# Keys of a pair of batches in one group of 512 columns, and context split a tile ahead, in a cross-attention, self-attention and expert kernel

## What is computed

```
x = x + cross_attention(layernorm(x), ctx, ctx)          # 16 heads of 16
x = x + self_attention(layernorm(x))                     # rms norm, rope, sigmoid weights
x = x + experts(layernorm(x))                            # top 1 of 8, capacity 160

q = layernorm(x) @ Wq.T + bq;  k = ctx @ Wk.T + bk;  v = ctx @ Wv.T + bv
cross_attention = softmax(q k^T) v @ Wo.T + bo
experts: logits = tokens @ gate_w + gate_b; expert = argmax; position = running count
         gelu(tokens @ w1 + b1) @ w2 + b2, times the gate's probability
```

## Time and profile before

| | |
|---|---|
| median of 3 runs (lowest to highest) | 1187.33 us (1187.31 to 1187.4) |
| the profiled execution: time, span | 1189.84 us, 1187.6 us |
| busy: TensorE, its weight loads | 1096.9 us (92%), 923.9 us (78%) |
| busy: VectorE, ScalarE, GpSimd | 896.2 us (75%), 809.6 us (68%), 252.5 us (21%) |
| scores of slot 0 start: tile 1, 4, 18, 30 | 48.34, 145.54, 592.50, 975.30 us |
| granted TensorE clock, 145.5 to 1007.2 us | 1.00 (2.4 GHz) |
| keys, 1536 matmuls of 256 columns | 216.3 us busy, 291 ns each |
| ScalarE's copy of keys, 256 of 128x256; of values, 128 of 128x512 | 484 ns each; 625 ns each |

### The profile page before, as it was taken

The page is one execution under the profiler, slowest core; times in us unless marked ns, Lnnn a source line. Parts: engine busy times, 40 slices in busy tenths (PEclk is TensorE's granted clock), DMA queues, the critical chain, the costliest instruction groups (busy, mean ns, idle before and its releaser), DMA issues. The chain is left out here.

```text
span 1187.6 us, 42401 instructions
## 1 busy us (share of the span) xinstructions
PE 1096.9 (92%) x16905; PEld 923.9 (78%) x16905; DVE 896.2 (75%) x2654; ACT 809.6 (68%) x2441; POOL 252.5 (21%) x565
## 2 busy tenths in 40 slices
PE   6899999999999999999999999999999999863996
PEld 5678788877878888888888878878888887742996
DVE  5768888888888888888888888888888888741121
ACT  5667777777777777777787777777777777621221
POOL 0001221222222222222222222222122222222111
PEclk9889999999999999999999999999999999955999
DMA  5443411222212211121111111112111211001573
GB/s 134 115 109 101 163 51 55 62 63 59 60 56 58 60 42 57 49 57 58 51 42 55 55 56 56 56 56 57 42 51 51 53 56 34 15 10 34 171 250 109
DMA packets 71922, 82.26 MB, mean 69 GB/s; under 512 B 16987, under 2 KB 50732, under 8 KB 71728
## 3 DMA queue, kind: packets, MB, share of 16 engines
q1 hardware_dynamic: 65280, 75.19, 21.6%
q0 software_dynamic: 3200, 3.71, 0.9%
q10 hardware_dynamic: 3248, 0.66, 0.3%
HBM read 64.79 MB, written 16.56 MB: 68 GB/s over the span
## 5 line engine op out<-in xcount | busy, mean ns | idle before, releaser
L721 ACT ACTIVATE prob<-score,nmx 128x257 f32<-128x257 f32 x512 | 236.2, 476 | 124.0 <-DVE nmx L929 124.0
L393 PE MATMUL kps<-ctx_p,wk_p 128*128 128x256 f32 x1536 | 216.3, 291 | 0.2 <-issue 0.2
L403 PE MATMUL vps<-wv_p,ctx_p 128*128 128x256 f32 x1536 | 213.5, 289 | 0.0
L393 PEld LDWEIGHTS kps<-ctx_p,wk_p 128*128 128x128 f32 x1536 | 196.9, 193 | 18.2 <-issue 15.5
L929 DVE TENSOR_REDUCE nmx<-score 128x2 f32<-128x514 f32 x256 | 165.2, 687 | 59.9 <-PE score L423 59.9
L403 PEld LDWEIGHTS vps<-wv_p,ctx_p 128*128 128x128 f32 x1536 | 193.1, 192 | 0.9
L940 DVE TENSOR_SCALAR prob<-prob,rsum 128x256 f32<-128x256 f32 x512 | 165.0, 365 | 9.1
L1255 POOL TENSOR_TENSOR rstd<-ve,const 128x1 f32<-128x1 f32 x64 | 53.0, 829 | 497.4 <-DVE ve L983 276.2
L439 PE MATMUL score<-const,prob 128*128 128x128 f32 x1024 | 148.9, 279 | 6.6 <-DVE prob L940 4.6
L439 PEld LDWEIGHTS score<-const,prob 128*128 128x128 f32 x1024 | 112.8, 142 | 22.5 <-DVE prob L940 21.8
L739 ACT ACTIVATE ctx_p<-ctxT,nlast 128x256 fp32r<-128x256 f32 x256 | 119.6, 536 | 0.4 <-issue 0.4
(11 more groups left out here) (150 smaller groups left out, 1748.0 us busy)
## 6 DMA issues: line engine op xcount, KB each, us to landing
ctxT<-in_ctxT SPq DMA_DIRECT2D x128, 257.0 KB, 3.0
w<-in_w SPq DMA_DIRECT2D x16, 1024.0 KB, 8.6
xq<-in_x SPq DMA_DIRECT2D x32, 128.0 KB, 2.1
xr<-in_x SPq DMA_DIRECT2D x32, 128.0 KB, 2.4
qbd<-qkT SPq DMA_DIRECT2D x256, 16.0 KB, 1.8
out<-row SPq DMA_DIRECT2D x32, 128.0 KB, 2.0
slots<-row SPq DMA_DIRECT2D x10, 257.0 KB, 5.7
x_a<-slots SPq DMA_DIRECT2D x8, 129.0 KB, 2.1
```

Source lines behind the costliest of these rows:

```text
L393: last = mm(kps[:, c, :], wk_p[:, x, n, c * P:(c + 1) * P], ctx_p[:, g, y, n, :], start=(n, x) == (0, LO), stop=(n, y) == (C - 1, LO))
L403: last = mm(vps[:, c, :], ctx_p[:, g, x, n, c * P:(c + 1) * P], wv_p[:, y, n, :], start=(n, x) == (0, LO), stop=(n, y) == (C - 1, LO))
L721: last = af(prob[:, m, :], score[:, m, 0:S], ACT.Exp, bias=nmx[:, m:m + 1], scale=1.0, accum_out=esum[:, m:m + 1])
```

## The change

Keys: one group now holds a pair of batches and one chunk, six matmuls with 512 columns. Slots 0 and 1 make the two chunks of this tile's second pair, slots 2 and 3 those of the next tile's first pair. ScalarE evacuates each with one operation. The context parts have a slot for each of four batches, and in slot j the parts of batch j of the next tile are made. The context loads go out correspondingly earlier, and on SyncE's queue they stand behind the loads of x, one of the two behind the qbd copies. ScalarE's copy `y2T` moves ahead of the copy of the values, and VectorE's `choose` behind `norm_x_apply` and `probT`.

```diff
-        ctx_p = sb("ctx_p", [P, 2, 2, C, SM], F32R)
+        ctx_p = sb("ctx_p", [P, 2, C, TB, SM], F32R)
-        kT = sb("kT", [P, 2, C, S])
+        kT = sb("kT", [P, 2, C, 2, S])
-        kps, vps = ps("kps", [P, C, SM]), ps("vps", [P, C, D])
+        kps, vps = ps("kps", [P, 2 * SM]), ps("vps", [P, C, D])
...
 SyncE
-                sp.wait_ge(s["ctx_parts"], floor0(TB * t + 2 * r - 2))
+                sp.wait_ge(s["ctx_parts"], floor0(TB * (t - 1) + 2 * r + 2))
...
             load_ctx(0, 1)
+            load_ctx(1, 0)
...
-                if q:
-                    load_ctx(i + 1, 0)
...
                 if once(i):
+                    load_ctx(1, 1)
                     load_weights()
...
-                if q:
-                    load_ctx(i + 1, 1)
+                if i <= T - 3:
+                    load_ctx(i + 2, 0)
                 if s1:
...
                     send_diag(lambda h: qkT[HD * h:HD * (h + 1), 0:C, :],
                               lambda h: qbd2[HD * h:HD * (h + 1), :, h, :], "qbd2_in")
+                if i <= T - 3:
+                    load_ctx(i + 2, 1)
...
 TensorE
+            def keys(t, r, c):
+
+                p = 2 * t + r
+                pe.wait_ge(s["ctx_parts"], 2 * p + 2)
+                pe.wait_ge(s["k_evac"], 2 * p + c)
+                for n in range(C):
+                    for x, y in PASSES:
+                        last = mm(kps[:, :], wk_p[:, x, n, c * P:(c + 1) * P],
+                                  ctx_p[:, y, n, 2 * r:2 * r + 2, :].rearrange("p j s -> p (j s)"),
+                                  start=(n, x) == (0, LO), stop=(n, y) == (C - 1, LO))
+                last.then_inc(s["k_done"], 1)
...
-            keys(0, 0)
+            keys(0, 0, 0)
             pe.wait_ge(s["wparts_done"], 2)
             values(0, 0)
+            keys(0, 0, 1)
...
-                    if ahead:
-                        keys(ta, ja)
+                    if xa and (j < 2 or q):
+                        keys(*((i, 1) if j < 2 else (i + 1, 0)), j % 2)
...
 ScalarE
+            def keys(t, r, c):
+                p = 2 * t + r
+                act.wait_ge(s["k_done"], 2 * p + c + 1)
+                act.wait_ge(s["s_done"], floor0(2 * (2 * p - 2)))
+                af(kT[:, r, c, :, 0:SM], kps[:, :].rearrange("p (j s) -> p j s", j=2), ACT.Identity, bias=b_k[:, c:c + 1],
+                   scale=1.0).then_inc(s["k_evac"], 1)
...
             context_hi(0, 0)
+            context_hi(0, 1)
...
-            keys(0, 0)
-            context_hi(0, 1)
+            keys(0, 0, 0)
+            context_hi(0, 2)
             values(0, 0)
+            keys(0, 0, 1)
+            context_hi(0, 3)
...
-                    if xa and (j < 2 or q):
-                        context_hi(*((i, j + 2) if j < 2 else (i + 1, j - 2)))
+                    if q:
+                        context_hi(i + 1, j)
...
+                    if j == 3 and s2:
+                        copy_rows(y2T[:, :, :], spare2_c, "y2t_ps", t2, "y2T_done")
                     if ahead:
                         values(ta, ja)
...
-                    if j == 3 and s2:
-                        copy_rows(y2T[:, :, :], spare2_c, "y2t_ps", t2, "y2T_done")
...
 VectorE
                     normalise(i, 0)
+                if q:
+                    norm_x_apply(i + 1)
+                if xa:
+                    probsT(i, 0)
                 if i >= 3:
                     choose(t2 - 1)
-                if xa:
-                    probsT(i, 0)
-                if q:
-                    norm_x_apply(i + 1)
...
-                    context_lo(i, 3)
+                if q:
+                    context_lo(i + 1, 1)
```

More of the change, by code:

```diff
@@ L383, in project_queries @@
                 last.then_inc(s["q_ps"], 1)
[L385 to L394, removed]
+            def keys(t, r, c):
[7 more added lines that the diff above has]
+                                  start=(n, x) == (0, LO), stop=(n, y) == (C - 1, LO))
                 last.then_inc(s["k_done"], 1)
             def values(t, j):
-                b, g = TB * t + j, j % 2
+                b = TB * t + j
                 pe.wait_ge(s["v_evac"], b)
@@ L424, in scores @@
                                   qz[rows, half, e, j, :, :].rearrange("p h q -> p (h q)"),
-                                  kT[rows, b_slot(j), e, :], start=True, stop=True)
+                                  kT[rows, j // 2, e, j % 2, :], start=True, stop=True)
                         if e and m % 2:
@@ L723, in exps, with context_hi @@
                     last.then_inc(s["exp_done"], 1)
[L725 to L739 removed]
+            def keys(t, r, c):
[4 more added lines that the diff above has]
+                   scale=1.0).then_inc(s["k_evac"], 1)
+            def context_hi(t, j):
+                b, r = TB * t + j, j // 2
+                act.wait_ge(ctx_in[r], 16 * C * (t + 1))
+                act.wait_ge(s["v_done"], floor0(b - TB + 1))
+                for c in range(C):
+                    last = af(ctx_p[:, HI, c, j, :], ctxT[:, r, c, j % 2, 0:SM], ACT.Identity, bias=nlast[:, c, b:b + 1], scale=1.0)
                 last.then_inc(s["ctx_hi"], 1)
@@ L1103, in _ @@
             context_lo(0, 0)
+            context_lo(0, 1)
             dve.wait_ge(s["bq_in"], 16 * 4)
@@ L1113, in _ @@
             v.tensor_copy(row[:, 2 * D + 1:ROW], k["sentinel"]).then_inc(s["slots_init"], 1)
-            context_lo(0, 1)
             dve.wait_ge(s["wkv_in"], 16 * 5)
-            v.tensor_copy(kT[:, :, :, SM:S], b_k[:, :].unsqueeze(1).unsqueeze(3).to_broadcast([P, 2, C, 1])
-                          ).then_inc(s["bk_done"], 1)
+            for r in range(2):
+                v.tensor_copy(kT[:, r, :, :, SM:S], b_k[:, :].unsqueeze(2).unsqueeze(3).to_broadcast([P, C, 2, 1])
+                              ).then_inc(s["bk_done"], 1)
+            context_lo(0, 2)
+            context_lo(0, 3)
             def body(i, half):
```

42 lines of the change are left out of this document (15 added, 27 removed).

## The result

The changed kernel takes 1167.37 us (median of 5 runs, 1165.84 to 1169.57), the kernel before in the same session 1187.33 us (1186.1 to 1190.12). The ratio is 0.983 [0.981, 0.985]: 20 us faster, where 29.6 were forecast. The time lies in the range of 1150 to 1173, the forecast of 1158 is 9 us too low.

The account below looks back on a forecast made before the run. TensorE was taken to set the pace, standing still twice a tile, for y2T and probT. Terms 19.5 + 14.2 + 1.1 + 0.8 - 2 - 4 = 29.6 us off 1187.3 gave 1157.7, say 1158 us; range 1150 to 1173.

Parts of the forecast that it names:

- The rows' copy: Slot 3: y2T copied ahead of the values ends the gate matmuls' wait, 0.65 us a tile, 30 tiles, 19.5 us.
- The choice: Slot 0: routing choice behind probT ends the weighted values' wait, 0.49 us for 29 tiles, 14.2 us; slot 1 slack 0.04.
- Wide keys: Six 512-column matmuls for twelve of 256: 0.035 us a tile, counting in slot 2 only, 1.1 us (0 to 5).
- The start: Before the first scores: added context parts and keys, weights behind one more context load, 4 us lost (1.5 to 6).
- The last tile: Slot 2 there has no keys; TensorE's wait before the transposes' second half shrinks, 0.8 us gained.
- The qbd copies: Their reader comes earlier, leaving 0.5 us of cover; late landings in 4 tiles cost 2 us (0 to 6).
- the rival built on the Trainium skill's sustained 131 ns a matmul: Keys in slot 2: 512-column matmuls take half the row's time, saving 14 us, 1144 us; chance 0.03.
- the qbd copies become the bound: Rival: the eighth copy lands at 593, not 592, in most tiles, losing 0.4 us a tile, 1170 us; chance 0.07.
- The range: Whole kernel: terms' bounds give 1150 to 1165 us, widened to 1150 to 1173 to reach the first two rivals.
- What would show it: Period 30.8 us, both waits gone; wrong over 31.3, transposes waiting over 0.1 in slot 1, or six matmuls under 1.3.
- stuck ahead of the rows' copy: Rival, slot 3: ScalarE waits for transposes arriving over 0.28 us late; at 2 us late, 1209 us; chance 0.05.
- no VectorE wait took either place: Denies the rival that a VectorE wait in slot 1 gives back slot 0's gain, 1172 us; chance 0.12.

Follow-up runs that it names:

- moves_only: The kernel before with only the two moves (y2T ahead of the values' copy, choice behind probT), keys and context as before: 1169.84 us, ratio 0.984.
- undo_rows_copy: The changed kernel with the rows' copy y2T put behind the values' copy again, the rest of the change kept: 1168.1 us, ratio 0.982 to the kernel before.

## Why the prediction was right, and where it was not

- *The rows' copy, 0.65 us a tile: right.* Slot 3 went from 8.84 to 8.19. 0.49 of it is the move (moves_only), 0.16 the shorter keys' copy, which the prediction had counted into the same step: `qz` stands 0.57 behind the keys' copy, not 0.50, and it still sufficed. That the move itself buys nothing in the time (undo_rows_copy) is the copies' doing, below.
- *The choice, 0.49: right.* Slot 0 went from 7.82 to 7.33, and nothing came back in slot 1: the 0.04 us of slack held (clean slot 1 went from 7.56 to 7.53).
- *Wide keys, 0.035 a slot in slot 2 alone: right in kind, low.* Slots 1 and 2 gave 0.03 and 0.06, over 27 tiles 2.4 us in place of 1.1. Six wide matmuls take 1.49 us, so the rival built on the Trainium skill's sustained 131 ns a matmul (TensorE: Matmul & The Clock Gate, Back-to-back issue gap) is out; the measurement decides.
- *The start, +4: right (+3.4), and for the reason given:* the last weight comes 3.6 us later.
- *The last tile, 0.8: right.* Its slot 2 went from 7.65 to 6.72 us.
- *The qbd copies, +2 (0 to 6): here the prediction failed.* Slot 0 lost 9.2 us more, over the upper bound of 6. The cover of 0.5 us was right: the copies' undisturbed landing is 8.3 and the reader comes at 8.8. What failed was "landing takes up to 3.5 us ... I charge 4 tiles": the count of late tiles was carried over from the kernel before, as if lateness were independent of the change. It isn't: what makes a copy late is TensorE's own instruction packet, which goes with TensorE's order of work and moved into the copies' way along with the reader. 14 tiles instead of 4, each at about 0.7 us (9.3 / 14). The charge of 0.5 us for a late tile was low by the prediction's own rows too: the longest landing of 3.5, less the usual 1.8 and the cover of 0.5, is 1.2. The rival "the qbd copies become the bound" (0.07, 1170) named this wait; it got the pace wrong, since the median landing stays at 1.8 us and a little under half of the tiles are hit, by up to 2 us. The measured 1167.4 lies between forecast and this rival, closer to the rival.
- *Tiles 1 to 3: near in sum (2.6 us gained, against some 1.9 in the terms: 2 x 0.65 + 0.49 + 0.1) by luck.* Slot 0 of tile 2 became 4.4 us shorter, since its wait of 2.1 us and the low clock behind it went; slot 2 of tile 3 became 3.5 longer, by a stop of 1.6 us and the low clock behind it. Neither was foreseen.
- *The range: it held by its reach, not by its terms.* "The terms' bounds give 1150 ... to 1165": 1167.4 is outside that, and inside 1173 only because the range was stretched to the rivals. Nor do the bounds give these ends: all at their worst they gain 14.4 + 12.2 - 6 - 6 = 14.6 us (1172.7), all at their best some 39.9 (1147.4).
- *What would show it:* the period was to be 30.8 and wrong over 31.3. It is 31.1 on average and 30.7 where no copy is late. TensorE's transposes wait for VectorE as little as before (5.1 us in the whole span, 4.6 before), and the six wide matmuls take 1.49 us.

Steps in the other rivals: ScalarE isn't stuck ahead of the rows' copy (the rows are there at 579.45, the copy starts at 579.84), and no VectorE wait took either place.

What stays open: half a packet's shift, which would have moved the late tiles at will; why the copy's last part takes 1.2 us from its last packet's start (8.63 to 9.80) in a late tile and 0.4 in one in time (7.92 to 8.29); and why slot 1 takes 7.61 us and not 7.53 in 12 of the 13 tiles whose slot 0 waited for a late copy, which makes up the 1.0 us more lost there.

## What to carry to other kernels

Before crediting a gain on the engine that sets the pace, list the transfers that it waits for next and their cover, and don't take the share of late ones from the trace of before: ask what makes them late, and whether that moves with the engine. A gain of 0.65 us a tile against a cover of 0.5 is a warning even if the median transfer is punctual. And the remedy is cheap: one line that puts 1.5 us of other work ahead of the reader was worth as much as a whole edit (11.6 us, 1167.37 to 1155.74).

And where a wait of 1.6 to 2.1 us stands in a stretch, read the granted clock behind it: here the low clock cost about as much again.

## What the runs showed of the hardware

- TensorE's instructions arrive over the same DMA engines as the data, 16,384 bytes at a time, 129 in 1166 us. A 16 KB copy from SBUF to SBUF lands 1.8 us after issue (median), and up to 3.7 in the changed kernel when such a packet falls upon it (3.9 over all traces). With a packet between issue and landing the eighth copy was late by 1.2 us or more in 105 of 105 tiles, and its last packet started 0.02 to 0.18 us after that packet's end.
- ScalarE takes 696 ns for the keys' 128x512 out of PSUM (with a bias, target in two pieces per partition, `kT`) and 619 for the values' (no bias, one piece, `vv`). No run tells the two differences apart, but the bias alone goes with more time too: in the kernel before the keys' 128x256 (bias, one piece) takes 484 ns, copies of 128x256 out of PSUM without one 385 to 452.
- Behind an idle stretch of TensorE of 2.12 us (before, until 80.12) and of 1.63 us (changed, until 128.99) the granted clock fell to 0.50, 1.2 GHz, for 81 to 85 and 130 to 132 us; twelve matmuls of 256 columns took 2.73 us (81.99 to 84.72) and not 1.53. Behind a stop of 0.89 us (undo_rows_copy) it stayed at 1.00.
- A float32 matmul written once runs as two, each with its weight load: 64 calls gave 128 rows, 22.78 us, and one instruction packet more.
